# Grouped graph network and expert layer: GpSimd's drain between the expert groups left out

## What is computed

```python
A = (adj != 0)
h = layernorm(x)
for i in range(3):
    m = h @ weight[i]
    aggr = einsum('bst,bsd->btd', A, m)
    h = gru_cell(aggr, h, w_ih, w_hh, b_ih, b_hh)
x = x + h
xf = layernorm(x).reshape(-1, 128)
H = gelu(xf @ W1 + b1)                       # 512 hidden features
probs = softmax(H @ Wg + bg)                 # 8 experts
e = argmax(probs)
out = x + probs[e] * (H @ Wd[e] + bd[e])     # each token by its one expert
```

## Time and profile before

| what | value |
|---|---|
| median of 3 runs | 539.69 us |
| the profiled execution's own time | 533.25 us |
| its span on the core | 531.5 us |
| PE busy | 482.2 us, 91% |
| VectorE busy | 359.4 us, 68% |
| ScalarE busy | 316.9 us, 60% |
| GpSimd busy | 360.0 us, 68% |
| mean granted TensorE clock | 0.945 of full |

### The profile page before, as it was taken

One profiled execution on the slowest core, in us unless ns is written; L12 is line 12 of the kernel. 1 busy time (PEld: TensorE's weight loads), 2 busy tenths in 40 slices (PEclk: granted clock), 3 DMA queues, 4 the chain that ended last, 5 costly groups with the idle time before them and its releaser, 6 DMA issues.

```text
span 531.5 us, 10215 instructions
## 1 busy us (share of the span) xinstructions
PE 482.2 (91%) x3047; PEld 392.7 (74%) x3047; DVE 359.4 (68%) x1152; ACT 316.9 (60%) x576; POOL 360.0 (68%) x346
## 2 busy tenths in 40 slices
PE   9999999999999999999997787869894999899791
PEld 5777888888888888888875564646774998698681
DVE  6789787888879888888787645646663646256341
ACT  3867977689777877878795554445422444242420
POOL 4488976899799988987776555554663543556544
PEclk9999999999999999999999777998996999799797
DMA  7512554121343311111111101113321324342110
GB/s 207 154 51 70 155 169 135 40 60 50 95 136 100 91 51 49 51 49 52 57 40 51 45 29 46 45 62 102 95 70 52 97 87 127 94 136 84 35 36 15
DMA packets 69525, 42.10 MB, mean 79 GB/s; under 512 B 9548, under 2 KB 66128, under 8 KB 69472
## 3 DMA queue, kind: packets, MB, share of 16 engines
q1 hardware_dynamic: 64048, 32.33, 21.3%
q0 software_dynamic: 4224, 8.92, 4.9%
q10 hardware_dynamic: 1200, 0.20, 0.2%
HBM read 16.90 MB, written 9.84 MB: 50 GB/s over the span
## 4 chain that ended last, share of the span: by engine, by line
PE 84%; issue 6%; ACT 6%; another core or an unknown queue 2%; DVE 1%; SPq 1%; DMA 0%; POOLq 0%; ACTq 0%
PE bank L614 18%; PE bank L616 17%; PE bank L615 17%; PE bank L858 12%; PE bank L645 8%; PE bank L781 3%; ACT adj_i L1072 3%; PE bank L834 1%; PE bank L737 1%; PE bank L632 1%; ACT xn L980 1%; PE bank L652 1%; PE bank L851 1%; SPq L372 1%
## 5 line engine op out<-in xcount | busy, mean ns | idle before, releaser
L1072 ACT ACTIVATE adj_i<-bank,b1c 128x512 f32<-128x512 f32 x132 | 84.5, 694 | 131.7 <-PE bank L616 74.9
L580 POOL DMA_INDIRECT sorted_rows<-xrow,pos x64 | 63.2, 988 | 53.6 <-issue 53.3
L858 PE MATMUL bank<-wd_sb,adj_i 128*128 x512 | 69.0, 292 | 13.0 <-issue 12.6
L477 POOL TENSOR_TENSOR diff<-hT,n_sb 128x512 f32<-128x512 f32 x48 | 67.3, 1403 | 17.9 <-ACT n_sb L959 17.8
L858 PEld LDWEIGHTS bank<-wd_sb,adj_i 128*128 128x128 f32 x512 | 65.7, 206 | 15.3 <-issue 15.0
L479 POOL TENSOR_TENSOR diff<-z_sb,diff 128x512 f32<-128x512 f32 x48 | 63.3, 1319 | 3.8
L614 PE MATMUL bank<-hT_hi,w_hi 128*128 128x512 f32 x132 | 60.5, 459 | 3.7 <-issue 3.3
L614 PE MATMUL bank<-ag_hi,wf_hi 128*128 128x512 f32 x144 | 59.0, 410 | 0.1
L591 POOL DMA_INDIRECT out_dram<-n_sb,home x32 | 32.0, 999 | 38.4 <-DVE n_sb L1618 28.2
L615 PE MATMUL bank<-ag_lo,wf_hi 128*128 128x512 f32 x144 | 57.0, 396 | 0.0
L616 PE MATMUL bank<-ag_hi,wf_lo 128*128 128x512 f32 x144 | 56.9, 395 | 0.0
(11 more groups left out here) (199 smaller groups left out, 1087.6 us busy)
## 6 DMA issues: line engine op xcount, KB each, us to landing
bands<-hT SPq DMA_DIRECT2D x192, 64.0 KB, 2.2
adj_i<-sorted_rows SPq DMA_DIRECT2D x64, 72.0 KB
xrow<-in_x_dram SPq DMA_DIRECT2D x16, 256.0 KB, 3.3
adj_i<-in_adj_dram SPq DMA_DIRECT2D x16, 256.0 KB, 3.8
wd_sb<-in_L_ffn_Wd_dram SPq DMA_DIRECT2D x8, 256.0 KB, 2.9
sorted_rows<-xrow,pos POOLq DMA_INDIRECT x64
A<-wd_sb SPq DMA_DIRECT2D x4, 256.0 KB
hT<-wd_sb SPq DMA_DIRECT2D x4, 256.0 KB
```

What stands on the lines that cost most here:

```text
L477: nc.gpsimd.tensor_tensor(diff[:, b, :], hT[:, g, :], n_sb[:, b, :], ALU.subtract).then_inc(diff_ok, 1)
L580: nc.gpsimd.indirect_dma_start(out=sorted_rows, out_offset=bass.IndirectOffsetOnAxis(ap=pos[:, g, j:j + 1], axis=0), in_=xrow[:, g * GR + ...
L858: last = nc.tensor.matmul(o, HT[:, sg % 2, k, j * P:(j + 1) * P], wd_sb[:, bass.ds(at + k * P, P)], start=(k == 0), stop=(k == KC - 1))
L1072: nc.scalar.activation(HT[:, hb, k, 0:n], HB[k][:, 0:n], ACT.Gelu, bias=b1c[:, k:k + 1]).then_inc(done, 1)
```

## The change

The drain in GpSimd's loop over the expert groups is left out, with the constant that placed it. GpSimd then goes from group 5's transfers straight to group 6's. All 132 indirect transfers (64 and 68) are followed by one drain only, the one that ends the program. No other instruction is added, removed or moved on any engine.

```diff
@@ -281,7 +281,6 @@
         FIRST_STEPS = 3
-        RETIRE = (6,)
         ACT_UNITS = 2
@@ -604,8 +603,6 @@
             for s in range(1, SGROUPS + 1):
                 step(s)
-                if s in RETIRE:
-                    nc.gpsimd.drain()
```

## The result

The changed kernel took 542.32 us (median; 538.95 to 546.31), beside 539.36 for the kernel before. The comparison of the two gives a ratio of 1.0117, 95% interval 1.0068 to 1.0167: 6.3 us slower (3.7 to 9.0). The profiled execution's own time is 538.95 us, its span 537.2, 5.7 more than the span before.

A forecast was written before the change was run, and what follows sets the result against it. TensorE (PE), busy for 91% of the span, was taken as the bound, with room on GpSimd. +4.58 for the last drain and -2.28 for the middle gave +2.30 on the 539.69 us median: 542.0 us, range 537.5 to 546.0.

The forecast's parts named there:

- The last drain (+4.58): At the program's end: the only remaining drain walks 100 transfers, 8.24 us alone instead of 3.66, paid in full.
- The line through two points: Drain cost read from the kernel before's two drains: 7.26 us behind 88 transfers, 3.66 behind 44.
- The choice of 100: Transfers the last drain finds: 132 less the first eight gate groups' 32, which share one semaphore; between ends 88 and 132.
- Rival 5: Past a length of 88, room is made one transfer at a time; last drain walks 110: 542.8 us, chance 0.05.
- rival 1: At the end, all 132 transfers still stand for the last drain, +7.20 there: 544.6 us, chance 0.20.
- rival 4: GpSimd empties the whole list once at issue, past 88; last drain finds 22, 1.86 us: 535.6 us, chance 0.08.
- The middle (-2.28): Expert groups 5 to 9: without the drain, groups 6 and 7 form no run of eight and PE's stall goes, -2.28 us.
- the four steps the usual 7.65: VectorE's steps from group 5 to 9 take the 7.65 us each of groups 2 to 5: 30.60 instead of 32.88.
- rival 2: In the middle, a pair still joins into a run of eight, gain 0: 544.3 us, or 546.9 with 132; chance 0.14.
- the company: PE's broken issue, left at 407.02, 461.26 and 496.66 us, stood beside ends of GpSimd runs of at least eight transfers.

The follow-up runs named there:

- the repeat: The changed kernel run once more unaltered, beside the kernel before: 544.27 us, ratio 1.0107 (1.0047 to 1.0167).
- the spaced: Changed kernel, but GpSimd waits before each group's transfers until those of the group before have landed: 494.67 and 495.26 us, ratios 1.0600 and 1.0619.
- the paired: Changed kernel, but GpSimd sends groups 2 to 13 two at a time, six runs of eight: 477.27 and 477.05 us, ratios 1.0232 and 1.0239.
- the same 16 drains: Kernel before with a drain after each of groups 0 to 15 instead of one: 534.87 us, ratio 0.9920; on another chip 498.06 us, 1.0685.

## Why the prediction was right or wrong

**Right in its number and its sign; of its two terms one held.** 542.0 was forecast and 542.32 measured, but the forecast was +2.3 us over the kernel before and the comparison says +6.3 (3.7 to 9.0). That the number is near is luck in part: the two medians lie only 2.96 us apart, and the -2.28 that did not come had pulled the forecast down to near that. By the ratio, which the repeat bears out (1.0107), the forecast of the difference was too low.

**The last drain (+4.58): right.** 8.24 us was forecast for 100 transfers, and 8.24 to 8.26 stood there in all seven profiles of the three kernels that have no drain but the last (the changed one, the spaced and the paired). The line through two points of the kernel before, 0.0818 us a transfer and 0.06 besides, held at three more counts: 5.63 at 68, 2.68 at 32, 9.23 and 9.21 at 112 (by the line 5.62, 2.68, 9.22). At 20 and 12 transfers the drain took a little more than the line (2.0, 2.21 and 1.66 against 1.70 and 1.04), and over four it ended with the landing, after 1.3 to 3.3 us. The choice of 100 was a guess from the semaphores, and the count is right: (8.25 - 0.06) / 0.0818 = 100. All seven have a gap of 0.51 us before the 114th transfer, 0.2 more than usual, and none of the kernels with a drain between has it (single profiles have such a gap elsewhere, at the 53rd, 93rd, 126th or 127th). The nearest reading is that 32 left there at once. That rests on one total alone, 132: no other total over 113 was tried. That they are g_early's 32, and go because they share a semaphore, was not tried either.

Rival 5, which let one transfer go at a time, would give 110 in the walk, its estimate midway between 88 and 132, or 113 if the odd gap before the 114th marks its limit; the measured 100 excludes both, and the 8.25 us exclude rival 1 (10.86) and rival 4 (1.86). The drain's whole record was one of the prediction's signs, 9.4 us for 100. It was 11.20, because 2.94 of it lay before the last transfer's end and not the 1.20 carried over from the kernel before; only the time behind the last transfer is a measure of the walk.

**The middle (-2.28): wrong.** The step that failed is "I give the four steps the usual 7.65: 30.60 instead of 32.88", taken as a gain of the whole program. The shown parts came: group 6's first transfer without its wait, no issue gaps at 457 to 461. The four steps took 31.62 us in the profile after and 30.19 in the repeat (442.60 to 472.79 by VectorE's products), so their size was about right. But VectorE's group 9 came at 470.14 and not at the forecast 465.5, and the program as a whole gained nothing that shows. The two comparisons on chip A, 6.3 +- 2.7 and 5.8 +- 3.2 us, together give 6.1 +- 2.1; less 4.6 for the tail that leaves +1.5 +- 2.1 for everything else, which does not hold -2.28. On chip B it is 4.6 - 4.6 = 0 within 1.1 us.

What stood in its place is rival 2, to which I gave 0.14: another pair joins, the middle is worth 0, and 4.6 us are left. In the profile after, groups 3 and 4 came with 1.2 us between them and groups 9 and 10 with 0.3, PE was broken behind each, and there was no drain near. I read one execution's stall as the drain's doing because a run of eight stood beside it.

**What the stalls hang on is open.** On chip A the company was real. Count as a run transfers with pauses of up to 1.25 us, the expert groups' in it, and take PE's gaps of over 0.25 us within 3 us of its end: in the six profiles there, 15 of the 16 runs of at least eight had over 1 us of them, and 8 of the 74 shorter ones. By gaps marked "issue" alone it is 13 of 16 and 2 of 74. On chip B runs of 8 to 76 had none in any profile. So a run is not a cause by itself. Nor is PE alone in it. In the stall of the kernel before that I priced, VectorE stood too, and came back only 0.2 us after PE:

```profile
461.47 0.49 DVE L1614 TENSOR_TENSOR r_sb<-bank,bd_bc 128x128 f32<-128x128 f32 x2 [8.88 <-remote]
```

I had ruled a wait out because the only one for output transfers is VectorE's, for transfers long landed (group 8 waits for those of group 4, and by 441.49 us 2784 packets had ended, 32 each for 87 of the 88 transfers); what released VectorE here the profile does not name. The spaced and the paired kernel were made to tell this on chip A, and both times the set ran on chip B; there they can't. What the traces do show is where the chips part: ScalarE's timeline in the kernel before and, second fence, in the changed kernel on chip B.

```profile
285.37 0.97 ACT L980 ACTIVATE xn<-xrow,gshift 128x128 f32<-128x128 f32 x2
291.72 0.69 ACT L1072 ACTIVATE adj_i<-bank,b1c 128x512 f32<-128x512 f32 x1 [5.39 <-remote]
```

```profile
284.71 0.99 ACT L980 ACTIVATE xn<-xrow,gshift 128x128 f32<-128x128 f32 x2
285.80 1.39 ACT L1072 ACTIVATE adj_i<-bank,b1c 128x512 f32<-128x512 f32 x2
```

Up to here the two executions are 0.7 us apart. Then ScalarE stands for 5.39 us on one chip, some 5 us behind GpSimd's first indirect transfer (280.91), and not on the other; by the first expert group it is 36 us (VectorE's first product at 386.41 and 350.44). The first is the kernel before and the second the changed one, but the change lies over 150 us further on, so it does not make this difference. PE stands with it, for 4.7 to 5.5 us near 294 us, in all six profiles of chip A and in none of the eight of chip B. The indirect transfers themselves cost the DMA engines the same: 4.9% of 531.5 us is 26.0, and on the other chip the page has 5.5% of 469.6, 25.8.

## What to carry to other kernels

Here a GpSimd drain took 0.0818 us for each indirect transfer issued since the drain before, from 32 to 112 of them and with the packets of all but the last one through when the count starts, and 8.25 us, as for 100, behind 132 (transfers of 128 rows, the only size tried). So price it by its count. Ask which drain stands where nothing else runs: the one that ends the program did in all 14 profiles. Put a drain earlier only where GpSimd has idle time left to catch up before its last transfer; the same 16 drains gave 0.8% on the chip where PE had the stalls told of above, and cost 6.9% where it had none of them. And don't price a stall that one profile shows beside a suspect: first see in a second execution of the same kernel whether it stays where it was.

## What was not expected of the hardware

- The same program with the same data took 538 us on one chip and 466 and 467 on two others, with less than 1 us of difference up to 285 us into it. On chip A the granted clock stands at 0.50 of full in eight stretches of the kernel before, each of 6.8 to 10.2 us, and PE had stood idle for 1.4 to 4.0 of the 6.8 us ahead of each: one, 459.3 to 466.1, begins within the stall. The mean was 0.945, and 0.63 in the step behind the stall. In the changed kernel on chip B it is 1.00 in all three windows above, and 0.50 only from 462.1 us to the end; PE's last matmul ended at 456.92.
- With 132 transfers and no drain between, one gap is 0.51 us instead of 0.30, before the 114th, and the last drain takes as long as over 100. My estimate is that 32 transfers left the count there, for 0.2 us, where a drain over 32 took 2.68: less than a tenth. It rests on this one total, and it was not tried to bring the last drain's count down that way.
- A drain over four transfers that had been issued just before took 1.3 to 2.4 us in 59 of 65 cases and 2.6 to 3.3 in the other six; where the landing is on record, it ended 0.2 us after it.
